# Fourier convolution slots cut into 30 ticks, with copies first on ScalarE, one more tap on TensorE and a split gelu

## Chip, cores and metric

The kernel runs on one core of a Trainium2 chip. The metric is the device time of one execution in microseconds. The whole network is one launch; the change touches one of its layers.

## The reference, cut to what matters

The network normalises and adds four layers in turn. The third, a Fourier convolution on an image of 2 x 64 x 256 x 256, is the one that matters here:

```python
x = jnp.einsum('bchw,oc->bohw', x, w_in)                      # 64 -> 384 channels
xf = jnp.fft.rfft2(patches_of_8x8(x)) * fft_filter
x = irfft2(xf)                                                # back to pixels
x = lax.conv_general_dilated(x, w_dw, padding=[(1, 1), (1, 1)], feature_group_count=C)   # 3x3, each channel alone
x1, x2 = jnp.split(x, 2, axis=1)
x = jax.nn.gelu(x1, approximate=False) * x2
return jnp.einsum('bchw,oc->bohw', x, w_out)                  # 192 -> 64 channels
```

Its result is added to its input (the residual).

## The kernel before, in words

**The work.** `fft_layer` (from line 1341) goes over 32 row blocks `r` of 8 image rows, and in each over the two images `b`: 64 **slots** `s = 2r + b`. The 384 channels lie in three blocks `oc` of 128, and a slot's 8 rows in two halves `h` of 4 rows, so the 3x3 convolution of a slot has six **units** `u = 3h + oc`, each 128 channels x 1024 pixels. The nine taps of a unit are shared out: TensorE adds the first one or two into a PSUM buffer `p_c` (two buffers, by the parity of the unit) with diagonal weights, VectorE adds the last five, one instruction each (line 1810), the fifth into `acc`, ScalarE multiplies the remaining ones into `ta` (line 1709), and GpSimd adds those to `acc` (line 1910). `N_PE = (1, 1, 2)` gives TensorE's number of taps by channel block; ScalarE has 3, 3 and 2, so 16 taps per slot.

**Around the units.** On TensorE, a row block is transposed (`turn`, 4 groups `g`), and each group brought to frequencies (`to_freq`), with ScalarE's copies `copy_ht` and `copy_ft` behind them; one PSUM buffer `p_q` serves these steps and the output products. For the next slot, `widen` (8 steps `p`) multiplies by `w_in` into the one buffer `p_f`, VectorE's `filter_` (line 1816) multiplies by the filter into one of two `v`, `from_freq` (16 steps `j`) brings it back to pixels in the one buffer `p_i`, and ScalarE's `place` (line 1688) copies that into `zb`, the padded image block. `widen(p)` waits for filter p - 1, `from_freq(j)` for filter j // 2 and for `place(j - 1)`. `carry` copies the two last rows of a block to the top of the next.

**Gate and output.** ScalarE's `gelu(s, h)` (lines 1719 and 1720) applies the gelu to channel block 0 and to half of block 2 into `ge`, once GpSimd has finished the sums of unit 3h + 2; GpSimd's `gate` (lines 1915 and 1919) multiplies them by the other channels; TensorE's `project` (two parts per slot) multiplies by `w_out`, and VectorE adds the residual (line 1832) and takes statistics for the next normalisation (line 1846). VectorE's last tap of a unit waits, before it overwrites `acc`, until the gate that read it is done.

**The order.** Each engine has its own program, written out by hand. TensorE and ScalarE go through 24 ticks per slot; tables such as `CONV_AT`, `BACK_AT` and `TURN_AT` say at which tick a step is issued. A tick is a place in the program, not a time: an engine executes in order and stands at the first wait that isn't met. VectorE goes through the slot's 30 taps and puts filters, residuals and statistics between them by `FILTER_N`, `RESIDUAL_N` and `STATS_N`. All turns and Fourier steps of the next row block lie in the slot with b = 0. GpSimd's order is: sums of unit 5 of the slot before, sums of unit 0, the gate of the slot before's second half, sums of units 1, 2, 3, gate of the first half, sums of unit 4. SyncE issues, in order and by row block, the load of the block after next, the store of the last one and the loads of its residual rows; the store waits for VectorE's residuals.

Of the kernel before, what the change touches and what calls it, by code (L numbers as in the profile page):

```python
# [1340 lines left out]
def fft_layer(nc, dram, bn2, bn3, H, W):  # L1341
# [3 lines left out]
    NR = H // P8  # L1345
# [11 lines left out]
    N_PE = (1, 1, 2)  # L1357
# [6 lines left out]
    with ExitStack() as ctx:  # L1364
# [53 lines left out]
        added = sem("act_tap_added")  # L1418
        ge_done = sem("gelu_done")
# [11 lines left out]
        def A(s, u):  # L1431

            n = [len(T_ACT[i % OC]) for i in range(6)]
            return s * sum(n) + sum(n[:u]) if s < NS else NS * sum(n) + (s - NS) * sum(n[:3]) + sum(n[:u])
# [88 lines left out]
        def _(pe):  # L1523
# [4 lines left out]
            def turn(r, g):  # L1528
                if g == 0:
                    pe.wait_ge(hn_done, r + 1)  # L1530
                    ahead(pe, xo_done, r * 4 - 4)
# [35 lines left out]

            def conv(s, b, u):

                h, oc = u // OC, u % OC  # L1570
                if u == 0:
                    if s < NS:
                        pe.wait_ge(zi_done, s * NJ + NJ)
                    else:
                        pe.wait_ge(edge, s - NS + 1)
                ahead(pe, tapped, (U(s, u) - 1) * ND)
                n = 2 if rows_of(s) == HR else 1
                for i in range(n):
                    rows = min(2, rows_of(s))
                    for t, (dy, dx) in enumerate(T_PE[oc]):  # L1580
                        y = h * HR + 2 * i + dy
                        last = nc.tensor.matmul(p_c[odd(s, u)][:, i * 512:i * 512 + rows * W], diag[:, oc, t, :],  # L1582
                                                zb[b][:, oc, y:y + rows, dx:dx + W],
                                                start=(t == 0), stop=(t == len(T_PE[oc]) - 1))
                last.then_inc(pc_ps, 1)
# [10 lines left out]
            def project(s, b, row, i):  # L1596
# [6 lines left out]
                if i == 0:  # L1603
                    pe.wait_ge(a_done, G(s, 0) + 1 if len(parts) == 2 or parts[0][1] == 0 else G(s - 1, 1) + 1)
                    if b == 0 and row is not None:
                        pe.wait_ge(q_done, (row + 1) * (2 * NG) + 2 * NG)
# [8 lines left out]
            def slot(r, b, s, first=False, no_next=False, no_row=False):  # L1615
                nb, ns = 1 - b, s + 1
                rows_left = r < NR - 1
                for j in range(TICKS):
                    if j in CONV_AT:
                        conv(s, b, CONV_AT[j])  # L1620
                    if not no_next and j in WIDEN_AT:
                        widen(ns, r + b, nb, WIDEN_AT[j])
                    if not first and j in PROJECT_AT:
                        project(s - 1, nb, r if rows_left else None, PROJECT_AT.index(j))
                    if not no_next:
                        if j in BACK_AT:
                            from_freq(ns, BACK_AT[j])
                        if j == NEXT_AT:
                            conv(ns, nb, 0)
                    if b == 0 and not no_row:  # L1630
                        if j in TURN_AT:
                            turn(r + 1, TURN_AT[j])
                        if j in FREQ_AT:
# [666 lines left out]
```

## Time and profile before

| | |
|---|---|
| three runs, median (lowest to highest) | 19279.74 us (19274.17 to 19281.36) |
| the profiled execution | 19279.87 us, its span 19278.1 us |
| VectorE busy, whole span | 18044.9 us, 94% |
| GpSimd busy | 17264.4 us, 90% |
| TensorE matmuls busy | 13115.2 us, 68% |
| ScalarE busy | 11279.7 us, 59% |
| VectorE's taps (line 1810), all | x1560 into `p_c`, mean 1274 ns; x390 into `acc` |
| GpSimd's additions (line 1910) | x1040, 2424.4 us, mean 2340 ns |
| ScalarE's taps (line 1709) | x1040, 1169.2 us, mean 1129 ns |
| TensorE's tap records (line 1582) | x2064, 993.2 us, mean 615 ns |
| ScalarE's copies into `zb` (line 1688) | x1024, 523.8 us, mean 512 ns |

The layer runs from about 15450 to 18890 us of the span; a longer Mamba layer lies before it and an 8x8 transform layer behind it. A busy time is the time in which an engine's instructions were in execution; the rest is waiting. A matmul of 512 float32 columns stands as two records in the trace. In the order of time, a bracket behind a row gives the idle time before it and what ended it.

### The profile page before, as it was taken

Reading aid. Unit: us, or ns where it says so; the run is one execution under the profiler, and the core shown is the slowest. Engines: PE = TensorE matmul, PEld = TensorE weight load, DVE = VectorE, ACT = ScalarE, POOL = GpSimd, SP = SyncE. Lnnn points to the kernel's source line nnn. Section 1 sums busy time; section 2 is a strip of 40 time slices with the busy share of each in tenths; the row PEclk is TensorE's granted clock in tenths of the full one; section 3 lists DMA queues with packets and bytes.
Section 4 is the critical chain, followed back from the end, with each engine's and each line's share of the span. In section 5 each row is a group of like instructions: output and inputs, shape, how many; then the busy total and the mean of one; then the engine's idle time right before and its main releaser. Section 6 shows DMA issues by size and latency. Waiting matters only on the chain. (4 is left out here: it accounts for less than half of the span.)

```text
span 19278.1 us, 147925 instructions
## 1 busy us (share of the span) xinstructions
PE 13115.2 (68%) x45790; PEld 4732.6 (25%) x45790; DVE 18044.9 (94%) x11642; ACT 11279.7 (59%) x12399; POOL 17264.4 (90%) x7417
## 2 busy tenths in 40 slices
PE   4876666666666666666666666666666678888885
PEld 2321111111111111111111111111111144444444
DVE  5989999999999999999999999999999979999996
ACT  1116666666666666666666666666666556666663
POOL 3989999999999999999999999999999969999991
PEclk8997777777777777777777777777777789999997
DMA  4335555555555555555555555555555511111114
GB/s 125 114 107 136 140 135 136 136 139 139 137 135 135 139 139 138 135 135 138 139 137 136 135 137 139 138 136 135 136 139 139 126 30 27 33 33 31 29 29 145
DMA packets 616198, 2249.23 MB, mean 117 GB/s; under 512 B 74881, under 2 KB 92147, under 8 KB 591091
## 3 DMA queue, kind: packets, MB, share of 16 engines
q1 hardware_dynamic: 610146, 2232.63, 44.9%
q10 hardware_dynamic: 5265, 7.14, 0.1%
q8 instruction: 368, 6.03, 0.1%
q14 instruction: 419, 3.43, 0.1%
HBM read 990.77 MB, written 174.96 MB: 60 GB/s over the span
## 5 line engine op out<-in xcount | busy, mean ns | idle before, releaser
L1324 POOL TENSOR_TENSOR h<-h,c_bc 128x1024 f32<-128x1024 f32 x4096 | 9603.0, 2357 | 791.6 <-DVE h L1280 746.2
L1280 DVE TENSOR_TENSOR_SCAN h<-da,state,px 128x1024 f32<-128x1024 f32 x3072 | 7210.1, 2347 | 109.6
L1151 ACT ACTIVATE da<-d_bc,a_neg 128x1024 f32<-128x1024 f32 x3072 | 3492.9, 1144 | 2615.9 <-DVE h L1280 2587.7
L1005 PE MATMUL py<-h,ysel 128*32 128x512 f32 x16384 | 2743.3, 802 | 2548.8 <-POOL h L1324 2548.5
L1274 DVE TENSOR_TENSOR px<-px,du_bc 128x1024 f32<-128x1024 f32 x3072 | 3783.7, 1232 | 312.6 <-PE px L991 89.1
L1910 POOL TENSOR_TENSOR acc<-acc,ta 128x1024 f32<-128x1024 f32 (+1 forms) x1040 | 2424.4, 2340 | 398.6 <-DVE acc L1810 295.4
L1316 POOL TENSOR_TENSOR xs<-du_bc,b_bc 128x1024 f32<-128x1024 f32 x1024 | 2409.9, 2353 | 0.0
L1280 DVE TENSOR_TENSOR_SCAN h<-px,state,xs 128x1024 f32<-128x1024 f32 x1024 | 2316.9, 2326 | 0.0
L1810 DVE SCALAR_TENSOR_TENSOR p_c<-zb,w_dw,p_c 128x1024 f32<-128x1024 f32 (+1 forms) x1560 | 1986.7, 1274 | 43.7 <-PE p_c L1582 11.2
L991 PE MATMUL px<-cf,bsel 32*128 32x512 f32 x3072 | 1335.6, 956 | 913.0 <-DVE h L1280 913.0
L1151 ACT ACTIVATE px<-d_bc,a_neg 128x1024 f32<-128x1024 f32 x1024 | 1144.2, 1117 | 894.4 <-DVE h L1280 880.1
L1005 PEld LDWEIGHTS py<-h,ysel 128*32 128x32 f32 x16384 | 509.8, 131 | 4376.6 <-POOL h L1324 3156.7
L1709 ACT ACTIVATE ta<-zb,w_dw 128x1024 f32<-128x1024 f32 (+1 forms) x1040 | 1169.2, 1129 | 302.8 <-POOL acc L1910 281.1
L1565 PE MATMUL p_i<-basis,v 128*128 128x128 f32 x6144 | 948.7, 291 | 437.4 <-ACT zb L1688 406.6
L962 PE MATMUL pm<-hx,w_tap 128*128 128x512 f32 x1024 | 765.8, 916 | 541.7 <-ACT hx L1072 541.7
L1582 PE MATMUL p_c<-zb,diag 128*128 128x512 f32 x2064 | 993.2, 615 | 150.2 <-DVE acc L1810 121.0
L674 POOL TENSOR_TENSOR apr<-apr 128x1024 f32<-128x1024 f32 x390 | 912.3, 2358 | 97.9 <-DVE apr L653 73.8
L1565 PEld LDWEIGHTS p_i<-basis,v 128*128 128x128 f32 x6144 | 777.2, 193 | 851.0 <-issue 550.9
L970 PE MATMUL pm<-hy,w_res 64*128 64x512 f32 x512 | 482.3, 1094 | 645.7 <-ACT u L1082 645.7
L1688 ACT ACTIVATE zb<-p_i 128x384 f32<-128x384 f32 x1024 | 523.8, 512 | 575.9 <-PE p_i L1565 564.3
L991 PEld LDWEIGHTS px<-cf,bsel 32*128 32x128 f32 x3072 | 329.4, 255 | 2029.0 <-issue 1409.7
L1112 ACT ACTIVATE yg<-pm,eps_c 128x1024 f32<-128x1024 f32 x256 | 285.1, 1114 | 919.3 <-PE pm L933 919.3
(219 smaller groups left out, 19476.1 us busy)
## 6 DMA issues: line engine op xcount, KB each, us to landing
d_bc<-delta SPq DMA_DIRECT2D x1024, 512.0 KB, 8.5
du_bc<-du SPq DMA_DIRECT2D x1024, 512.0 KB, 8.6
c_bc<-c_rows_dram SPq DMA_DIRECT2D x1024, 512.0 KB, 5.4
b_bc<-c_rows_dram SPq DMA_DIRECT2D x256, 512.0 KB, 8.1
hx<-x_dram SPq DMA_DIRECT2D x252, 256.5 KB, 6.3
st_x<-in_x_dram SPq DMA_DIRECT2D x32, 1024.0 KB, 4.9
ax<-in_x_dram SPq DMA_DIRECT2D x64, 512.0 KB, 3.4
xr<-x_dram SPq DMA_DIRECT2D x64, 512.0 KB, 6.1
```

The costliest lines, as they stand in the source:

```text
L991: last = nc.tensor.matmul(px[(t.par + q // 3 + q) % 2][:, cut], bsel[rows, q, :], cf[rows, cut], start=True, stop=True)
L1005: last = nc.tensor.matmul(py[32 * j:32 * j + 32, cut], ysel[:, :], h[:, (4 * q + j) % 8, cut], start=False, stop=(q == Q - 1))
L1151: nc.scalar.activation(out[:, :], d_bc[:, n % J, :], ACT.Exp, scale=a_neg[t.l][:, n:n + 1]).then_inc(da_done, 1)
L1274: nc.vector.tensor_tensor(out=x[:, :], in0=b[:, :], in1=du_bc[:, j, :], op=ALU.mult).then_inc(m1_done, 1)
L1280: nc.vector.tensor_tensor_scan(h[:, n % 8, PAD:T + PAD], a[:, :], x[:, :], state[:, 2 * t.l + t.b, n:n + 1], ALU.mult, ALU.add).then_inc(s ...
L1316: nc.gpsimd.tensor_tensor(out=xs[i][:, :], in0=du_bc[:, n % J, :], in1=b_bc[:, :], op=ALU.mult).then_inc(xs_done, 1)
L1324: nc.gpsimd.tensor_tensor(out=h[:, n % 8, 0:T], in0=h[:, n % 8, PAD:T + PAD], in1=c_bc[q % 2][:, :], op=ALU.mult).then_inc(m2_done, 1)
L1565: last = nc.tensor.matmul(p_i[:, c], v[j // 2 % 2][:, j % 2, c], basis[:, 1, :], start=True, stop=True)
L1582: last = nc.tensor.matmul(p_c[odd(s, u)][:, i * 512:i * 512 + rows * W], diag[:, oc, t, :], zb[b][:, oc, y:y + rows, dx:dx + W], start=(t ...
L1709: nc.scalar.activation(ta[odd(s, u)][t][:, 0:n * W].rearrange("p (y x) -> p y x", y=n), zb[b][:, oc, y:y + n, dx:dx + W], ACT.Identity, sc ...
L1810: nc.vector.scalar_tensor_tensor(out=out, in0=zb[b][:, oc, y:y + n, dx:dx + W], scalar=w_dw[:, oc, m:m + 1], in1=other, op0=ALU.mult, op1= ...
L1910: nc.gpsimd.tensor_tensor(out=acc[h][oc][:, c], in0=acc[h][oc][:, c], in1=ta[o][t][:, c], op=ALU.add).then_inc(added, 1)
```

## The change

The slot is cut into 30 ticks, one for each of VectorE's taps, and the tables are written anew. TensorE's tap matmuls are issued one at a time (`conv_piece`) between other steps instead of a unit at once. In a tick, ScalarE's `place` and the row block's copies now come ahead of its taps. `N_PE` is given by unit and TensorE takes a second tap for unit 4, which ScalarE and GpSimd give up (15 taps and additions per slot instead of 16). The gelu's two instructions are issued at two ticks, with a semaphore after the first that VectorE's tap into channel block 0 waits for instead of the gate. GpSimd's gate of the slot before stands behind the sums of unit 1 instead of unit 0. The fourth group of turn and Fourier step moves to the slot with b = 1. The core of the diff:

```diff
-    N_PE = (1, 1, 2)
+
+    N_PE = (1, 1, 2, 1, 2, 2)
...
-        TICKS = 24
-        CONV_AT = {4 * (u - 1) + 1: u for u in range(1, 6)}
-        NEXT_AT = 21
-        PROJECT_AT = (1, 4)
-        WIDEN_AT = {2 * p + 1: p for p in range(NP)}
-        BACK_AT = {j + 3: j for j in range(NJ)}
-        TURN_AT = {4 * g + 7: g for g in range(NG)}
-        FREQ_AT = {4 * g + 9: g for g in range(NG)}
-        CARRY_AT, GELU_BACK_AT, GELU_AT = 1, 5, 17
-        FILTER_N = {n: p for p, n in enumerate((3, 5, 8, 10, 13, 15, 18, 20))}
-        RESIDUAL_N, STATS_N = (3, 7), (4, 8)
+
+        TICKS = 6 * ND
+        CONV_AT = {0: (1, 0), 1: (1, 1), 5: (2, 0), 6: (2, 1), 7: (2, 2), 8: (2, 3), 10: (3, 0), 11: (3, 1),
+                   15: (4, 0), 16: (4, 1), 17: (4, 2), 18: (4, 3), 20: (5, 0), 21: (5, 1), 22: (5, 2), 23: (5, 3)}
+        NEXT_AT = 27
+        PROJECT_AT = (4, 9)
+        WIDEN_AT = {3 * p + 1: p for p in range(NP)}
+        BACK_AT = {3 * (j // 2) + 4 + j % 2: j for j in range(NJ)}
+
+        FIRST = 3
+        TURN_AT = ({13: 0, 19: 1, 25: 2}, {13: 3})
+        FREQ_AT = ({17: 0, 22: 1, 26: 2}, {16: 3})
+        TAP_AT = {2: (0, 0), 3: (0, 1), 4: (0, 2), 5: (1, 0), 6: (1, 1), 7: (1, 2), 9: (2, 0), 10: (2, 1), 14: (3, 0), 16: (3, 1),
+                  18: (3, 2), 21: (4, 0), 22: (4, 1), 26: (5, 0), 27: (5, 1)}
+        CARRY_AT, GELU_BACK_AT, GELU_AT = 1, (11, 12), (23, 24)
+        FILTER_N = {3 * p + 3: p for p in range(NP)}
+        RESIDUAL_N, STATS_N = (6, 12), (7, 13)
...
                 for j in range(TICKS):
-                    if j in CONV_AT:
-                        conv(s, b, CONV_AT[j])
                     if not no_next and j in WIDEN_AT:
                         widen(ns, r + b, nb, WIDEN_AT[j])
+                    if not no_next and j in BACK_AT:
+                        from_freq(ns, BACK_AT[j])
                     if not first and j in PROJECT_AT:
...
+                    if j in CONV_AT:
+                        conv_piece(s, b, *CONV_AT[j])
+                    if not no_next and j == NEXT_AT:
+                        conv(ns, nb, 0)
+                    if r < NR - 1 and j in TURN_AT[b]:
+                        turn(r + 1, TURN_AT[b][j])
+                    if r < NR - 1 and j in FREQ_AT[b]:
+                        to_freq(r + 1, FREQ_AT[b][j])
...
                 for j in range(TICKS):
-                    if j % 4 < NA:
-                        tap(s, b, j // 4, j % 4)
+                    if not no_next and j - 1 in BACK_AT:
+                        place(ns, nb, BACK_AT[j - 1])
+                    if r < NR - 1:
+                        if b == 0 and j == 0:
+                            norm(r + 1)
+                        if j - 1 in TURN_AT[b]:
+                            copy_ht(r + 1, TURN_AT[b][j - 1])
+                        if j - 1 in FREQ_AT[b]:
+                            copy_ft(r + 1, FREQ_AT[b][j - 1])
                     if not first and j == CARRY_AT:
                         carry(s - 1, nb)
...
+                    if j in TAP_AT:
+                        tap(s, b, *TAP_AT[j])
+                    if not first and j in GELU_BACK_AT:
+                        gelu(s - 1, 1, GELU_BACK_AT.index(j))
+                    if j in GELU_AT:
+                        gelu(s, 0, GELU_AT.index(j))
...
-                    ahead(dve, a_done, prev)
+
+                    ahead(dve, a_done if oc else ge_half, prev)
...
                 sums(s, 0)
+                sums(s, 1)
                 if not first:
                     gate(s - 1, 1)
-                for u in (1, 2, 3):
+                for u in (2, 3):
                     sums(s, u)
                 gate(s, 0)
                 sums(s, 4)
```

## Rows read from the trace of the kernel before

**Rows 1.** busy time by stretch: us, busy (x instructions), PEclk, DMA share, GB/s

```profile
17000.00:18000.00 1000.00, 829.06 (x4253) 453.30 (x4252) 919.70 (x821) 652.00 (x815) 918.89 (x391) 0.99 0.12 32
18728.00:18732.00 4.00, 3.60 (x4) 1.17 (x4) 3.93 (x4) 1.47 (x2) 3.71 (x3) 0.50 0.00 0
```

**Rows 2.** DVE's order of time (start us, us): the first taps of four slots

```profile
15555.97 3.94 DVE L1810 SCALAR_TENSOR_TENSOR p_c<-zb,w_dw,p_c 128x1024 f32<-128x1024 f32 x3 [8.44 <-PE p_c L1582]
...
17042.42 3.93 DVE L1810 SCALAR_TENSOR_TENSOR p_c<-zb,w_dw,p_c 128x1024 f32<-128x1024 f32 x3
...
17090.35 2.61 DVE L1810 SCALAR_TENSOR_TENSOR p_c<-zb,w_dw,p_c 128x1024 f32<-128x1024 f32 x2
...
18778.91 5.26 DVE L1810 SCALAR_TENSOR_TENSOR p_c<-zb,w_dw,p_c 128x1024 f32<-128x1024 f32 x4
```

**Rows 3.** waits, 15600 to 18800: us in total, times, longest

```profile
DVE v L1816 <- PE p_fr L1556: 206.9, 194, 1.6
...
POOL acc L1910 <- DVE acc L1810: 145.5, 62, 5.3
```

**Rows 4.** DVE's order of time, one stretch in detail

```profile
17035.92 5.26 DVE L1810 SCALAR_TENSOR_TENSOR p_c<-zb,w_dw,p_c 128x1024 f32<-128x1024 f32 x4
17041.22 1.28 DVE L1810 SCALAR_TENSOR_TENSOR acc<-zb,w_dw,p_c 128x1024 f32<-128x1024 f32 x1
...
17046.26 0.95 DVE L1816 TENSOR_TENSOR v<-p_fr,filt 128x768 f32<-128x768 f32 x1
17047.12 1.28 DVE L1810 SCALAR_TENSOR_TENSOR p_c<-zb,w_dw,p_c 128x1024 f32<-128x1024 f32 x1
17048.31 0.68 DVE L1832 TENSOR_TENSOR fxo<-p_qo,fxr 128x512 f32<-128x512 f32 x1
17048.91 1.27 DVE L1810 SCALAR_TENSOR_TENSOR acc<-zb,w_dw,p_c 128x1024 f32<-128x1024 f32 x1
```

**Rows 5.** POOL's order of time: gate products and additions

```profile
17034.61 2.37 POOL L1915 TENSOR_TENSOR ge<-ge,acc 128x1024 f32<-128x1024 f32 x1
...
17039.50 19.57 POOL L1910 TENSOR_TENSOR acc<-acc,ta 128x1024 f32<-128x1024 f32 x8
17059.02 2.37 POOL L1915 TENSOR_TENSOR ge<-ge,acc 128x1024 f32<-128x1024 f32 x1
```

**Rows 6.** ACT's order of time: first half of a gelu

```profile
17078.72 1.05 ACT L1719 ACTIVATE ge<-acc 128x1024 f32<-128x1024 f32 x1
```

**Rows 7.** PE's order of time, two stretches

```profile
17038.96 0.60 PE L1535 MATMUL p_qo<-f_mats,hn 128*128 128x128 f32 x4
17039.73 1.98 PE L1582 MATMUL p_c<-zb,diag 128*128 128x512 f32 x4 [0.17 <-ACT zb L1688]
17041.64 1.09 PE L1545 MATMUL p_qo<-basis,ht 128*64 128x128 f32 x16
...
17045.43 1.08 PE L1590 MATMUL p_qo<-ge,w_out 128*64 128x512 f32 x4
...
17047.44 0.92 PE L1556 MATMUL p_fr<-w_in,ft 64*128 64x384 f32 x4
...
17051.17 0.94 PE L1565 MATMUL p_i<-basis,v 128*128 128x128 f32 x6
17051.94 3.60 PE L1582 MATMUL p_c<-zb,diag 128*128 128x512 f32 x8
17055.47 0.92 PE L1556 MATMUL p_fr<-w_in,ft 64*128 64x384 f32 x4
17056.31 0.94 PE L1565 MATMUL p_i<-basis,v 128*128 128x128 f32 x6
17057.94 0.91 PE L1565 MATMUL p_i<-basis,v 128*128 128x128 f32 x6 [0.69 <-ACT zb L1688]
...
18728.40 3.78 PE L1582 MATMUL p_c<-zb,diag 128*128 128x512 f32 x4 [3.35 <-DVE acc L1810]
```

**Rows 8.** DMA issues, 15500 to 18800: KB each, median us to landing

```profile
fxr<-x_dram SPq DMA_DIRECT2D x62, 512.0 KB, 8.7
```

More of the change, by code:

```diff
@@ L1418, in fft_layer @@
         added = sem("act_tap_added")
+        ge_half = sem("gelu_first_half_done")
         ge_done = sem("gelu_done")
@@ L1431, in A @@
         def A(s, u):
-            n = [len(T_ACT[i % OC]) for i in range(6)]
+            n = [len(t) for t in T_ACT]
             return s * sum(n) + sum(n[:u]) if s < NS else NS * sum(n) + (s - NS) * sum(n[:3]) + sum(n[:u])
@@ L1530, in turn @@
                     pe.wait_ge(hn_done, r + 1)
-                    ahead(pe, xo_done, r * 4 - 4)
+                if g in (0, FIRST):
+                    ahead(pe, xo_done, r * 4 - 4 + (2 if g else 0))
                 ahead(pe, q_done, r * (2 * NG) + 2 * g)
@@ L1566, in from_freq, with conv_piece, pieces_of @@
                 last.then_inc(i_ps, 1)
-            def conv(s, b, u):
[L1570 to L1585, printed above, removed]
+            def conv_piece(s, b, u, k):
+                h, oc = u // OC, u % OC
+                if k == 0:
+                    if u == 0:
+                        if s < NS:
+                            pe.wait_ge(zi_done, s * NJ + NJ)
+                        else:
+                            pe.wait_ge(edge, s - NS + 1)
+                    ahead(pe, tapped, (U(s, u) - 1) * ND)
+                n = len(T_PE[u])
+                i, t = k // n, k % n
+                rows = min(2, rows_of(s))
+                dy, dx = T_PE[u][t]
+                y = h * HR + 2 * i + dy
+                last = nc.tensor.matmul(p_c[odd(s, u)][:, i * 512:i * 512 + rows * W], diag[:, oc, t, :],
+                                        zb[b][:, oc, y:y + rows, dx:dx + W], start=(t == 0), stop=(t == n - 1))
+                if k == pieces_of(s, u) - 1:
+                    last.then_inc(pc_ps, 1)
+            def pieces_of(s, u):
+                return len(T_PE[u]) * (2 if rows_of(s) == HR else 1)
+            def conv(s, b, u):
+                for k in range(pieces_of(s, u)):
+                    conv_piece(s, b, u, k)
             def product(parts, i, w):
@@ L1604, in project @@
                     pe.wait_ge(a_done, G(s, 0) + 1 if len(parts) == 2 or parts[0][1] == 0 else G(s - 1, 1) + 1)
-                    if b == 0 and row is not None:
-                        pe.wait_ge(q_done, (row + 1) * (2 * NG) + 2 * NG)
+                    if row is not None and (b or row < NR - 1):
+                        pe.wait_ge(q_done, row * (2 * NG) + 2 * NG if b else (row + 1) * (2 * NG) + 2 * FIRST)
                 ahead(pe, xo_done, O(s, i))
@@ L1648, in _ @@
                     slot(r, b, r * 2 + b)
-            slot(NR - 1, 0, NS - 2, no_row=True)
+            slot(NR - 1, 0, NS - 2)
             slot(NR - 1, 1, NS - 1, no_next=True)
@@ L1693, in tap @@
                 h, oc = u // OC, u % OC
-                if t >= len(T_ACT[oc]):
-                    return
                 if u == 0 and t == 0:
@@ L1760, in _ @@
                     slot(r, b, r * 2 + b)
-            slot(NR - 1, 0, NS - 2, no_row=True)
+            slot(NR - 1, 0, NS - 2)
             slot(NR - 1, 1, NS - 1, no_next=True)
             carry(NS - 1, 1)
-            gelu(NS - 1, 1)
+            for part in range(2):
+                gelu(NS - 1, 1, part)
             for b in range(2):
                 for u in range(OC):
-                    for t in range(NA):
+                    for t in range(len(T_ACT[u])):
                         tap(NS + b, b, u, t)
-                gelu(NS + b, 0)
+                for part in range(2):
+                    gelu(NS + b, 0, part)
         @block.vector
@@ L1784, in _ @@
             for oc in range(OC):
-                for t, tap in enumerate(T_PE[oc]):
+                for t, tap in enumerate(TAPS[:max(N_PE)]):
                     n = TAPS.index(tap)
@@ L1905, in sums @@
                 pool.wait_ge(tapped, (U(s, u) + 1) * ND)
-                for t in range(len(T_ACT[oc])):
+                for t in range(len(T_ACT[u])):
                     pool.wait_ge(t_done, A(s, u) + (t + 1))
```

56 lines of the change are left out of this document (17 added, 39 removed).

## The prediction, made before the changed kernel was built or run

> **What bounds the kernel now.** The change lies in the Fourier stage alone, so I read that stage. The table by stretch shows VectorE (DVE) and GpSimd (POOL) both busy 92% of the time there, with TensorE (PE) busy 83% and its granted clock at 0.99 of full speed [rows 1]. DVE's slots of 30 taps give the pace: 63 slots pass between the first tap and the first tap of the last slot, 3222.94 us or 51.16 each [rows 2]. A slot with b = 1 takes 47.93; the one with b = 0, which also turns the next row block into frequencies on PE, takes the rest of a pair, 54.4. The waits say where that goes: DVE waits 206.9 us for the widening matmul before a filter, about 3.3 per slot, and POOL 145.5 for DVE's last tap of a unit [rows 3]. So PE is late, not full: it stands in its program order, behind products, Fourier steps and pieces that themselves wait for a copy of ScalarE (ACT), while DVE stands still.
>
> **What each engine needs without waits.** DVE: four dependent taps take 5.30, so 1.325 each; a tap followed by something independent costs 1.19, a filter 0.86, a residual or a statistic 0.60 [rows 4]. Before, 12 of the 30 taps have an independent follower, so 14.3 + 18 x 1.325 + 8 x 0.86 + 4 x 0.60 = 47.4, which is the b = 1 slot less its short wait. After, filters stand before taps 3, 6, ... 24, residuals behind taps 6 and 12: 17 taps have such a follower, and the sum is 20.2 + 17.2 + 6.9 + 2.4 = 46.8 (-0.6). POOL: eight additions take 19.52, 2.44 each, a gate's two products 4.89 [rows 5]. Before, 16 additions and two gates are 48.8, more than DVE's 47.4: POOL alone would have capped any better order. Taking the second tap of unit 4 to PE removes one addition: 46.4. ACT, busy 65% [rows 1], loses one tap; splitting the gelu adds no instruction (two of 1.05 stay two [rows 6]), so both cost nothing by themselves. PE gains two pieces of 0.88 per slot, 1.8 us.
>
> **PE in the new order, by hand from the slot's first tap.** Prices from start to start [rows 7]: T (transpose) 0.77, F (to frequencies) 1.03 (its row 1.09 less the overlap), P (product) 2.01, W (widen) 0.84, B (back) 0.77 ahead of a piece and 0.86 elsewhere (its 0.94 less 0.08, the overlap that W shows with 0.92 and 0.84), C (tap piece) 3.53 / 4 = 0.88. Where a B has only its sibling's copy on ACT ahead of it, it starts 1.63 after that sibling. No row shows single pieces between other operations. From above one costs 0.96 (1.91 for two ahead of F, halved), from below I allow as much the other way, 0.80, since less weight of its own might be waited for; I take 0.88, the row with most pieces, and keep 0.08 x 14 = 1.1 us per slot, up or down, for the range.
> W1 can't start before filter 0, which starts at 3.84, has ended: 4.8. From there to the end of unit 5's pieces PE has, in order, 7 W (5.9), 14 B of which 11 run into a piece (10.9), 14 C (12.4), 2 P (4.0), and T and F once (1.8): 35.1. The chain of copies adds waits: with b = 1 I find 0.1 at B7, nothing where W or C lies between, and 0.8 at B11. So unit 5 is ready at 4.8 + 35.1 + 0.9 = 40.8, where DVE without waits would want it at 40.3 (tap 25). With b = 0 there is a second T and F before that point; T falls into B11's wait, F adds 1.0: 41.8. Everything earlier is in time: unit 2 at 15.3 for tap 10 at 16.1, W3 by 17.2 for the filter at 18.6, unit 4 at 31.6 for 32.3. Behind tap 25, B14, B15, T, F and the next slot's first pieces end at 47.9 for 48.3.
> So DVE waits 0.5 with b = 1 and 1.5 with b = 0: slots of 47.3 and 48.3, **95.6 us per pair**.
>
> **POOL's and ACT's queues.** Gelu's second half of the first part waits on ACT behind place 12, frequency copy and place 13, and is done at 43.3 with b = 0 and 41.6 with b = 1; POOL would reach its gate at about 40.7 and 41.4. It stands up to 2.6 us, and what is queued behind it, unit 4's sums, comes by 2.6 later into the next slot, where ACT's taps of unit 0 wait for them and place 0 stands behind those taps. In the next slot tap (0,2) then ends at 6.9, place 0 starts there, and B1, for which PE is free only at 8.6 (P), loses nothing. POOL's work of 46.4 fits into 47.3 with 0.9 over, so the delay is caught up. The back gate behind the second sums starts at about 24, its gelu is done at 22. DVE now needs only the first half of gelu for channel block 0 (tap 19): ready at 20.5, wanted at 31. The residual moves from taps 3 and 7 to 6 and 12; the store and the load of the next residual rows on SP's queue issue behind it, some 10 us later, and the load lands 8.7 us after its issue [rows 8], with 38 us until it is read: hidden. The other loads keep their place by row block. T3 and F3 move to the b = 1 slot, where their price is in the sum above; W6 reads them after they are copied.
>
> **Sum.** After: 63 slots at 47.8 = 3012, the first 1.3 less (no products, no backlog). Before: 3223. Gain 211 + 1 = 212 us. Two more diagonal weights are built once, under 1 us. The last slot has neither filters nor a next slot and the tail runs as before: nothing. The profiled execution took 19279.9, practically the median of the three runs (19279.7): 19280 - 212 = 19068; I say 19070.
>
> **A rule on the clock.** After PE stood 3.35 us idle ahead of a slot's second unit, four tap records took 3.78 us in some slots, where two pieces usually take 1.91 [rows 7]; in that stretch the granted clock is 0.50, which is 1.2 GHz [rows 1]. If the new order kept one such stretch in every pair and it fell on the path, 31 x 1.9 = 59 us would be added: 19130. The Trainium skill (TensorE: Matmul & The Clock Gate, "What's actually happening") says that the gate throttles after idleness and that activity releases it; the trace agrees. By that rule the new order, whose longest idle stretch of PE is some 2 us in my walk, would lose the slow stretches, and the sum stays at 19070.
>
> **The rivals.** (1) DVE's own time: if pieces cost 0.8 and no copy makes B wait, unit 5 is ready by 40.3 and each slot takes 46.8: 63 x 4.36 = 275, 19005 us. For it: my sum is over by only 0.5 with b = 1. Against it: F and T with b = 0. (2) PE dearer: at 0.96 a piece and a few more copy waits each slot has 1.1 to 2 us more, 48.9 to 49.8: 19140 to 19195. For it: PE would be busy nine tenths of the slot in strict order, so little absorbs it. (3) No change within 0.2%: PE must add 3 us to a slot, twice that. (4) Slower: the ring through POOL and ACT. Gate end, sums of unit 4 (4.9), ACT's taps (0,1) and (0,2) 2.1 (each about a gelu half), place 0, B1, PE's order up to B13, place 13, gelu's second half, gate (4.9). My steps give 48.5 for b = 0 and 46.1 for b = 1, 94.5 per pair, just under the forecast's 95.6; it closes first if ACT's taps stand ahead of copies. It decides beyond 95.6 and makes the kernel slower beyond 102.3, which needs 0.5 us for each of 8 pairs of B in both slots: 52 per slot, +53 us, 19333. For it: before, ACT's copies already wait in this way. Against: in the new order copies come first. That the change doesn't do what it says is unlikely: order and counts are fixed by hand.
>
> **Chances.** Forecast 0.5 (19030 to 19120), (1) 0.18, (2) 0.2, (3) 0.06, (4) 0.06. A measurement of this kernel can tell about 0.2% (39 us) from no change. The range takes in (1) and (2): 19000 to 19200. Faster 0.88, same 0.06, slower 0.06.
>
> **What would show it.** POOL's additions fall from 1040 by 64, PE's tap records rise from 2064 by 256. Right: DVE's waits for the widening matmul nearly gone, and instead a wait at tap 25 for the pieces of unit 5, about 0.5 and 1.5 us by turns; slots of 47.3 and 48.3; POOL's wait moved from DVE to gelu. Wrong: DVE waiting in several places of a slot, slots above 49, or no DVE wait at all and 46.8.

## The result, and the profile after

The changed kernel took 19105.06 us (median of four runs, 19099.55 to 19115.74), the kernel before 19279.95 beside it: a ratio of 0.9911, 95% interval 0.9896 to 0.9926. That is 175 us less where 210 were forecast, inside the range of 19000 to 19200. The profiled execution took 19099.55 us, its span 19097.7, which is 180.4 less than the span before.

The page of the changed kernel, its first part and three of its groups:

```profile
PE 13183.2 (69%) x46046; PEld 4686.6 (25%) x46046; DVE 17998.3 (94%) x11644; ACT 11214.6 (59%) x12335; POOL 17116.8 (90%) x7353
...
L1926 POOL TENSOR_TENSOR acc<-acc,ta 128x1024 f32<-128x1024 f32 (+1 forms) x976 | 2273.0, 2339 | 230.3 <-DVE acc L1826 135.8
...
L1826 DVE SCALAR_TENSOR_TENSOR p_c<-zb,w_dw,p_c 128x1024 f32<-128x1024 f32 (+1 forms) x1560 | 1983.2, 1271 | 135.7 <-PE p_c L1591 112.2
...
L1591 PE MATMUL p_c<-zb,diag 128*128 128x512 f32 x2320 | 1179.8, 607 | 115.8 <-DVE acc L1826 91.7
```

GpSimd's additions fell by 64 to 976, TensorE's tap records rose by 256 to 2320: the change does what it says. VectorE's busy time hardly moved (before 18044.9). What moved is its idle time. The stretches that answer to [rows 1], then the waits of the layer that answer to [rows 3]:

```profile
17000.00:18000.00 1000.00, 904.58 (x4510) 462.21 (x4510) 956.52 (x868) 665.35 (x833) 923.20 (x393) 0.99 0.13 33
17056.00:17060.00 4.00, 4.00 (x16) 1.64 (x14) 3.96 (x5) 2.64 (x4) 3.86 (x3) 0.57 0.00 0
```

```profile
POOL ge L1931 <- ACT ge L1733: 135.2, 69, 4.2
...
DVE p_c L1826 <- PE p_c L1591: 101.3, 73, 2.3
PE p_fr L1565 <- DVE v L1832: 100.8, 60, 1.7
POOL acc L1926 <- DVE acc L1826: 23.9, 3, 15.2
DVE v L1832 <- PE p_fr L1565: 2.5, 10, 0.3
```

VectorE is busy 957 us of 1000 instead of 919. Its 194 waits for the widening matmul, 206.9 us, have shrunk to 10 with 2.5 us; in their place it waits for tap pieces, 101.3 us. GpSimd's 145.5 us for VectorE have gone and it now waits 135.2 for the gelu. TensorE is busy 90% of the stretch, before 83%.

VectorE in order of time: the first taps of four slots, the filter 0 of one, and all its waits in two neighbouring slots (from 17001.35 with b = 0, from 17050.25 with b = 1):

```profile
15545.61 3.94 DVE L1826 SCALAR_TENSOR_TENSOR p_c<-zb,w_dw,p_c 128x1024 f32<-128x1024 f32 x3 [8.44 <-PE p_c L1591]
...
17001.35 3.93 DVE L1826 SCALAR_TENSOR_TENSOR p_c<-zb,w_dw,p_c 128x1024 f32<-128x1024 f32 x3
17005.19 0.95 DVE L1832 TENSOR_TENSOR v<-p_fr,filt 128x768 f32<-128x768 f32 x1
...
17043.75 5.26 DVE L1826 SCALAR_TENSOR_TENSOR p_c<-zb,w_dw,p_c 128x1024 f32<-128x1024 f32 x4 [2.05 <-PE p_c L1591]
...
17050.25 3.93 DVE L1826 SCALAR_TENSOR_TENSOR p_c<-zb,w_dw,p_c 128x1024 f32<-128x1024 f32 x3
...
17067.26 2.61 DVE L1826 SCALAR_TENSOR_TENSOR p_c<-zb,w_dw,p_c 128x1024 f32<-128x1024 f32 x2 [0.84 <-PE p_c L1591]
17070.13 0.96 DVE L1832 TENSOR_TENSOR v<-p_fr,filt 128x768 f32<-128x768 f32 x1 [0.26 <-PE p_fr L1565]
...
17093.01 5.26 DVE L1826 SCALAR_TENSOR_TENSOR p_c<-zb,w_dw,p_c 128x1024 f32<-128x1024 f32 x4 [1.13 <-PE p_c L1591]
...
18601.38 5.26 DVE L1826 SCALAR_TENSOR_TENSOR p_c<-zb,w_dw,p_c 128x1024 f32<-128x1024 f32 x4
```

The first slot with b = 0 takes 48.90 and waits once, 2.05 us at tap 25. An undisturbed slot with b = 1 takes 47.68 and waits 0.83 there: 96.58 us per pair. The slot at 17050.25 takes 49.26, because it also waits at tap 10 (unit 2) and at a filter. Ten of the 63 slots are such, each 1.6 us longer. The kernel before has ten long slots too, all with b = 0, mostly 55.48 against 53.96. From the first tap to the first tap of the last slot 3055.77 us pass (before 3222.94, [rows 2]), a gain of 167.2. The other 13.2 of the 180.4 lie outside the slots: the first tap comes 10.4 earlier, and from the last slot's first tap to the end 2.9 less pass. Most of the 10.4 is not the change's, as the paragraph on the sum shows.

### The profile page after: what moved, and what is told of

Its sections match the earlier page's. It is cut to its first block and busy times, and to the rows that moved or that the text cites. A ratio compares the mean times of both kernels' runs of the same rounds, so it can differ in the third digit from the quotient of the medians.

```text
span 19097.7 us, 148278 instructions
## 1 busy us (share of the span) xinstructions
PE 13183.2 (69%) x46046; PEld 4686.6 (25%) x46046; DVE 17998.3 (94%) x11644; ACT 11214.6 (59%) x12335; POOL 17116.8 (90%) x7353
## 5 line engine op out<-in xcount | busy, mean ns | idle before, releaser
L1926 POOL TENSOR_TENSOR acc<-acc,ta 128x1024 f32<-128x1024 f32 (+1 forms) x976 | 2273.0, 2339 | 230.3 <-DVE acc L1826 135.8
L1591 PE MATMUL p_c<-zb,diag 128*128 128x512 f32 x2320 | 1179.8, 607 | 115.8 <-DVE acc L1826 91.7
L1720 ACT ACTIVATE ta<-zb,w_dw 128x1024 f32<-128x1024 f32 (+1 forms) x976 | 1074.1, 1127 | 142.4 <-POOL acc L1926 120.5
```

Of the source, the lines that this page charges most:

```text
L1720: nc.scalar.activation(ta[odd(s, u)][t][:, 0:n * W].rearrange("p (y x) -> p y x", y=n), zb[b][:, oc, y:y + n, dx:dx + W], ACT.Identity, sc ...
L1926: nc.gpsimd.tensor_tensor(out=acc[h][oc][:, c], in0=acc[h][oc][:, c], in1=ta[o][t][:, c], op=ALU.add).then_inc(added, 1)
```

## The experiments

Each kernel starts from the changed one unless it says otherwise, and all compute the whole output. "Slots" are the intervals from a slot's first tap to the next slot's first tap, b = 1 and then b = 0, those that occur most; "in the slots" is the sum of all 63, to be held against the changed kernel's 3055.8. A slot is called disturbed when it is longer than most of its kind. The kernel before took 19281.24, 19274.01 and 19281.92 (medians of seven) beside the three groups of runs: so medians of one kernel differ by 8 us from group to group. A figure of one run is named as such.

**1. The first product one tick earlier.**

```diff
-        PROJECT_AT = (4, 9)
+        PROJECT_AT = (3, 9)
```

> The first product moves from tick 4 to tick 3, ahead of the second widening step. Theory A (the slot is set by PE's program from filter 0 to the pieces of unit 5; ahead of it PE stands idle for 1.68 us, waiting for that filter): the product fills the idle time and unit 5 is ready about 1.7 us earlier. DVE's wait at tap 25 falls from 0.83 to 0 with b = 1 and from 2.05 to about 0.4 with b = 0; undisturbed slots of 46.8 and 47.2 us instead of 47.68 and 48.90, and the slots that are 1.6 us longer because PE's clock halved become rarer. Time about 19010 to 19030. Theory B (the ring through POOL's gate, its sums, ACT's taps and the first copy sets the pair): pairs stay at 96.6 us, or fall at most to 94.5 and PE waits elsewhere; time 19040 to 19105.

Measured: 19081.01 (19077.37 to 19084.99), ratio 0.9898 (0.9881 to 0.9914). Undisturbed slots 47.43 and 48.65: the wait at tap 25 shrank by 0.25, not by the length of a product. TensorE, in order of time:

```profile
17021.77 1.13 PE L1591 MATMUL p_c<-zb,diag 128*128 128x512 f32 x2 [0.49 <-DVE acc L1826]
```

TensorE came earlier to unit 4's first piece and then stood there until VectorE had ended unit 2, whose `p_c` buffer unit 4 reuses. In the changed kernel that piece starts at 17026.08, 0.33 after VectorE could free the buffer (unit 2's last tap starts at 17024.41, and from such a tap's start to the piece behind it 1.34 pass elsewhere). So the stretch that sets the slot begins at unit 2's end, and only what lies behind it, up to unit 5's last piece, counts. In the slots 27.9 us went: 62 by 0.25 are 15.5, and the disturbed slots gave 12.4, as there are five instead of ten, and each is 0.7 to 0.9 longer instead of 1.6. The profiled executions differ by only 18.3, since here the first tap came at 15556.04, 10.4 later than in the changed kernel's, though nothing ahead of it differs. Theory A expected 46.8 and 47.2 and had missed this second start of the stretch.

**2. The tap back to ScalarE and GpSimd.**

```diff
-    N_PE = (1, 1, 2, 1, 2, 2)
+    N_PE = (1, 1, 2, 1, 1, 2)
...
-                   15: (4, 0), 16: (4, 1), 17: (4, 2), 18: (4, 3), 20: (5, 0), 21: (5, 1), 22: (5, 2), 23: (5, 3)}
+                   15: (4, 0), 16: (4, 1), 20: (5, 0), 21: (5, 1), 22: (5, 2), 23: (5, 3)}
...
-                  18: (3, 2), 21: (4, 0), 22: (4, 1), 26: (5, 0), 27: (5, 1)}
+                  18: (3, 2), 21: (4, 0), 22: (4, 1), 24: (4, 2), 26: (5, 0), 27: (5, 1)}
```

> The changed kernel with the second tap of unit 4 given back from PE to ACT and POOL; all else stays. PE has 1.8 us less work per slot, POOL 2.44 more. Theory A (POOL's own work would cap the new order without this part): the wait at tap 25 goes (PE is 1.8 us earlier), but POOL needs 48.8 per slot, plus what it waits for; slots of at least 48.8 by both parities, 97.7 per pair against 96.6, and DVE waits through ACT's late taps and copies. Time 19140 to 19170. Theory B (only PE's order mattered): slots of 47.0 to 47.4, time about 19050.

Measured: 19151.20 (one run), slots of 48.05 to 51.3, 49.0 on average, against GpSimd's own 48.8. Its additions stand there as x5 and x11 per slot with next to no idle time:

```profile
17010.26 12.22 POOL L1926 TENSOR_TENSOR acc<-acc,ta 128x1024 f32<-128x1024 f32 x5
17022.43 2.36 POOL L1931 TENSOR_TENSOR ge<-ge,acc 128x1024 f32<-128x1024 f32 x1
17024.87 2.37 POOL L1935 TENSOR_TENSOR ge<-ge,acc 64x1024 f32<-64x1024 f32 x1
17027.32 26.90 POOL L1926 TENSOR_TENSOR acc<-acc,ta 128x1024 f32<-128x1024 f32 x11
```

GpSimd is the bound in this order. The run is 46 us above the changed kernel, but 12 of the difference of the profiled executions lie ahead of the first tap, in work that is the same in both; in the slots the tap is worth 31.0 us, and behind the last slot's first tap 8.6 more, some 40 in all.

**3. The back gate ahead of unit 1's sums, as before.**

```diff
                 sums(s, 0)
-                sums(s, 1)
                 if not first:
                     gate(s - 1, 1)
-                for u in (2, 3):
+                for u in (1, 2, 3):
```

> The changed kernel with GpSimd's gate of the slot before in front of the sums of unit 1 again. Theory A (a ring: gate, all of POOL's sums up to unit 4, ACT's taps of unit 0, the first copy, PE up to the second product, the gelu, the gate again): 34.3 of POOL, 2.8 of ACT, 9.6 of PE, 4.5 of copies and gelu make 51.2 us, longer than the slot, so every slot takes about 51; time 19105 + 61 x 2.9 = about 19280, the place of the gate undoes the whole gain. Theory B (POOL has the slack to absorb a gelu 6 us late, since it is only moved in phase): slots stay at 47.7 and 48.9, time within 15 us of 19105.

Measured: 19486.47 (one run), slots 53.91 and 55.32, 381 us more. One round in order of time, GpSimd, ScalarE, VectorE:

```profile
17045.62 2.37 POOL L1931 TENSOR_TENSOR ge<-ge,acc 128x1024 f32<-128x1024 f32 x1 [5.58 <-ACT ge L1733]
```

```profile
17052.88 1.15 ACT L1720 ACTIVATE ta<-zb,w_dw 128x1024 f32<-128x1024 f32 x1 [5.33 <-POOL acc L1926]
```

```profile
17061.40 1.29 DVE L1826 SCALAR_TENSOR_TENSOR p_c<-zb,w_dw,p_c 128x1024 f32<-128x1024 f32 x1 [5.80 <-PE p_c L1591]
```

GpSimd stands for a gelu; its sums come late, so ScalarE's taps stand; the copies behind them come late, TensorE stands, and VectorE has no piece. ScalarE's waits for these sums, over the layer:

```profile
ACT ta L1720 <- POOL acc L1926: 459.4, 205, 5.3
```

The changed kernel has 117.6 there. The ring is real, and dearer than the 51 us per slot that I expected. Part of that is the clock: TensorE stands 4.78 us for a copy at 17054.58, the granted clock in 17052 to 17056 is 0.76, and nearly every slot has such a stretch. How much of the surplus it makes was not separated.

**4. Both halves of the gelu at one place.**

```diff
-                    if not first and j in GELU_BACK_AT:
-                        gelu(s - 1, 1, GELU_BACK_AT.index(j))
-                    if j in GELU_AT:
-                        gelu(s, 0, GELU_AT.index(j))
+                    if not first and j == GELU_BACK_AT[0]:
+                        for part in range(2):
+                            gelu(s - 1, 1, part)
+                    if j == GELU_AT[0]:
+                        for part in range(2):
+                            gelu(s, 0, part)
```

> The changed kernel with both halves of each gelu issued at the first half's tick. Theory A (the halves don't matter: what follows the gelu's end has slack or the copies lose about as much as the gate gains): the second half ends 0.5 us earlier in the tick of the copy of place 13, that copy starts up to 1 us later, DVE's wait at tap 25 grows by at most 0.5 us; time within 30 us of 19105. Theory B (the split is what keeps the copies in time): place 5 and place 13 come 1 us late, B6 and B14 with them, slots of 49.5 and more, time 19150 and above.

Measured: 19169.26 (one run), slots 49.26 and 49.49. Every slot with b = 1 but the first now has the slow stretch; TensorE in order of time and the same stretch in the table:

```profile
16996.31 1.65 PE L1565 MATMUL p_fr<-w_in,ft 64*128 64x384 f32 x4 [2.13 <-DVE v L1834]
16997.89 1.65 PE L1574 MATMUL p_i<-basis,v 128*128 128x128 f32 x6
```

```profile
16996.00:17000.00 4.00, 3.69 (x12) 2.15 (x14) 3.96 (x5) 0.43 (x2) 3.51 (x2) 0.57 0.00 0
```

In the slots 58.5 us are lost. Those with b = 1 are 1.58 longer than undisturbed ones of the changed kernel, exactly as its own disturbed ones (49.26), so what they lose is the clock's share. Those with b = 0 are 0.59 longer: a copy of ScalarE now lies behind both halves, and TensorE stands 1.62 us for it. The other 10.7 us of the profiled execution lie ahead of the first tap (15556.26). The number is Theory B's; its mechanism made the smaller part.

**5. The tap alone, on the kernel before.**

```diff
-    N_PE = (1, 1, 2)
+    N_PE = (1, 1, 2, 1, 2, 2)
```

(with the tables of taps by unit instead of by channel block)

> The kernel before, with its 24 ticks and its order, and with only one part of the change: PE takes the second tap of unit 4, ACT and POOL give it up. Theory A (in the old order PE is late and POOL is only near its limit, so the tap pays nothing alone): PE has 1.8 us more in its b = 0 slot, POOL's slack goes unused; time between 19260 and 19320. Theory B (POOL's 16 additions were what held the old order): 2.4 us per slot less, time about 19130.

Measured: 19372.98 (one run) against 19274.01, 99 us slower, and more than either theory allowed; 98.8 of it lie in the slots. GpSimd has less to do and gains nothing by it; TensorE's longer program makes the widening matmul later. The waits that answer to [rows 3]:

```profile
POOL acc L1910 <- DVE acc L1810: 383.8, 117, 7.6
...
DVE v L1816 <- PE p_fr L1556: 297.6, 237, 2.9
```

The same tap that saves some 40 us in the new order costs 99 in the old one.

**6. All four turns and Fourier steps in the slot with b = 0.**

```diff
-        FIRST = 3
-        TURN_AT = ({13: 0, 19: 1, 25: 2}, {13: 3})
-        FREQ_AT = ({17: 0, 22: 1, 26: 2}, {16: 3})
+        FIRST = 4
+        TURN_AT = ({13: 0, 17: 1, 20: 2, 24: 3}, {})
+        FREQ_AT = ({15: 0, 19: 1, 22: 2, 26: 3}, {})
```

> The changed kernel with the fourth turn and Fourier step back in the slot with b = 0 (turns at ticks 13, 17, 20, 24, Fourier steps at 15, 19, 22, 26). Theory A (the slot's length is set by what PE has to do between the first piece of unit 4, which waits for DVE's unit 2, and the last piece of unit 5): in b = 0 that stretch grows by 1.8 to 2.5 us, undisturbed slots of 50.7 to 51.4; in b = 1 it shrinks by 1.0, the wait of 0.83 at tap 25 goes, 46.9; pairs of 97.6 to 98.3 against 96.6, time 19135 to 19160. Theory B (PE's total per pair decides): pairs of 96.6, time 19105.

Measured: 19115.66 (one run), slots 46.77 and 49.87, 96.64 per pair against 96.58. With b = 1 VectorE then waits for nothing, and the slot with b = 0 pays it back; ten slots with b = 1 are 1.33 longer. In the slots it is 4.0 us more, and the first two slots with b = 0 alone are 6.5 longer. Where the fourth group lies is worth nothing that shows. Theory A's account still held: with b = 0, TensorE's time from unit 4's first piece to unit 5's last is 17.58 (17040.91 to 17058.49) against 16.61 (17026.08 to 17042.69), 0.97 more, and the slot is 0.97 longer. Its 50.7 to 51.4 were too high, since the turns between pieces cost 0.44 from start to start (17046.97 to 17047.41) instead of 0.77 and waits for copies went.

**7. ScalarE's copies behind its taps and gelus in each tick.**

```diff
-                    if not no_next and j - 1 in BACK_AT:
-                        place(ns, nb, BACK_AT[j - 1])
...
                     if j in GELU_AT:
                         gelu(s, 0, GELU_AT.index(j))
+                    if r < NR - 1:
...
+                    if not no_next and j - 1 in BACK_AT:
+                        place(ns, nb, BACK_AT[j - 1])
```

> The changed kernel with ACT's taps and gelus ahead of its copies in each tick, as before. Theory A (the copies are what PE waits for, so taps in front of them lengthen PE's chain): most places come 0.5 to 1.1 us later, and the first ones wait for POOL's sums as well; B steps wait more, DVE waits for widening steps or pieces in several places, slots of 50 and more, time 19230 or above. Theory B (ACT has enough idle time for either order): less than 0.3 us per slot, time within 20 us of 19105.

Measured: 19343.85 (one run), slots 49.85 and 52.88, or 51.43 and 54.46 where disturbed; VectorE's waits for tap pieces 284.2 us. Without copies first the new tables are slower than the kernel before. The copies are late by themselves and not through the ring, for ScalarE's taps hardly wait for GpSimd's sums here (the changed kernel has 117.6, experiment 3 459.4):

```profile
ACT ta L1720 <- POOL acc L1926: 1.4, 9, 0.2
```

TensorE's waits for copies into `zb` ahead of a `from_freq` grow from 89.9 to 216.4 us.

**8. Each unit's pieces together, at the place of the first.**

```diff
-                        conv_piece(s, b, *CONV_AT[j])
+                        if CONV_AT[j][1] == 0:
+                            conv(s, b, CONV_AT[j][0])
```

> The changed kernel with each unit's pieces issued together at the tick of the first one, as before, and all else as changed. Theory A (what counts is the stretch of PE's program up to unit 5's last piece): unit 5's four pieces come ahead of W7, B12, F1 and B13, so the wait at tap 25 goes; W7 comes about 1 us late for its filter instead; slots of 47.7 to 48.0 by both parities, about 95.8 per pair against 96.6, time about 19085. Theory B (single pieces between the other steps are what keeps the widening steps in time, as the kernel before shows with its waits for them): filters wait in several places, slots above 49, time above 19130.

Measured: 19334.36 (one run), slots 50.36 and 52.15, every other one with b = 1 53.55; VectorE waits 247.5 us for the widening matmul, as before the change. A whole unit is 3.5 us in front of a step that VectorE wants. This is Theory B. Part of the loss is the clock: TensorE's falls in almost every slot, and the 16 long ones, 3.2 us longer each, are those in which it stays low for longest (0.50 in 17072 to 17076 of one).

**9. Unit 5's pieces a tick earlier, the first product too, the second Fourier step a tick later.**

```diff
-                   15: (4, 0), 16: (4, 1), 17: (4, 2), 18: (4, 3), 20: (5, 0), 21: (5, 1), 22: (5, 2), 23: (5, 3)}
+                   15: (4, 0), 16: (4, 1), 17: (4, 2), 18: (4, 3), 19: (5, 0), 20: (5, 1), 21: (5, 2), 22: (5, 3)}
...
-        PROJECT_AT = (4, 9)
+        PROJECT_AT = (3, 9)
...
-        FREQ_AT = ({17: 0, 22: 1, 26: 2}, {16: 3})
+        FREQ_AT = ({17: 0, 23: 1, 26: 2}, {16: 3})
```

> The changed kernel with three edits to PE's order: the first product at tick 3, unit 5's pieces one tick earlier (19 to 22, so ahead of B11 and B13), and the second Fourier step of b = 0 at tick 23, behind the last of these pieces. Theory A (the stretch from unit 4's first piece to unit 5's last sets the slot; e1 gained only 0.25 us per slot since that first piece waits for DVE's unit 2 and not for PE): the stretch is 0.8 shorter with b = 1 and 1.8 with b = 0; with e1's gain the waits at tap 25 of 0.83 and 2.05 go, both slots take DVE's own 46.8 to 46.9; time 19105 - 63 x 1.4 = about 19015. Theory B (POOL's gate and the ring through ACT set the pair by then): PE's gain is given back as POOL's and ACT's waits, slots of 47.2 or more, time above 19035.

Measured: 19031.33 (19021.75 to 19031.72), ratio 0.9874 (0.9857 to 0.989): 74 us below the changed kernel. The only wait of VectorE in a pair of slots, and the total over the layer:

```profile
17011.62 3.94 DVE L1826 SCALAR_TENSOR_TENSOR p_c<-zb,w_dw,p_c 128x1024 f32<-128x1024 f32 x3 [0.93 <-PE p_c L1591]
```

```profile
DVE p_c L1826 <- PE p_c L1591: 30.7, 32, 1.4
```

The wait at tap 25 is gone, a pair takes 94.56, and no slot has a stretch of low clock. In the slots it is 78.5 us less: 62.6 from the waits and 16 from the disturbed slots. That lies between the two theories (19015, or above 19035), as the next slot's unit 0 kept a wait. 2 x 46.8 + 0.93 is 94.5: what is left is VectorE's own time and one wait for the next slot's unit 0.

**10. As 9, with the third Fourier step behind the next slot's unit 0.**

```diff
-        FREQ_AT = ({17: 0, 23: 1, 26: 2}, {16: 3})
+        FREQ_AT = ({17: 0, 23: 1, 28: 2}, {16: 3})
```

> e9 with one more edit: the third Fourier step of b = 0 goes from tick 26 to tick 28, behind the next slot's first pieces. e9 has one wait of DVE left, 1.04 us per pair, for these pieces. Theory A (it is the 1.03 us of this step): the wait goes, pairs of 93.5 us, which is DVE's own time; 31 x 1.04 = 32 us less than e9, 18990 to 19000. Theory B (POOL's and ACT's ring sets e9's 94.56 per pair, which is also the 94.5 of the prediction's sum for the ring): the wait moves elsewhere and the pair stays at 94.5, time 19020 to 19031.

Measured: 19062.89 (19052.87 to 19064.52), ratio 0.9886 (0.9869 to 0.9902), 31 us worse than 9; VectorE's wait grew to 2.31 in the slot read. TensorE in order of time there, and ScalarE:

```profile
17031.00 0.91 PE L1574 MATMUL p_i<-basis,v 128*128 128x128 f32 x6 [1.05 <-ACT zb L1701]
17032.82 3.41 PE L1591 MATMUL p_c<-zb,diag 128*128 128x512 f32 x4 [0.92 <-ACT zb L1701]
```

```profile
17037.52 0.60 ACT L1695 ACTIVATE ft<-p_qo 128x512 f32<-128x512 f32 x1 [3.73 <-PE p_qo L1554]
```

With the Fourier step gone from between them, TensorE stood twice for a copy, and its four records then took 3.41 us where they take 1.99 elsewhere. ScalarE, whose copy of that step stands ahead of its taps, waited 3.73. The step I took out had been filling a gap: in the nine slots with b = 0 that ran at full clock nothing was gained (47.74 against 47.78), and 21 others, with the clock low behind these waits (0.65 in 17032 to 17036), take 48.05 to 49.44, which is where the 31 us went. Neither theory had this.

**11. Three constant matmuls ahead of W1, in the idle time of 1.68 us.**

```diff
+                    if not first and j == 3:
+                        for _ in range(3):
+                            nc.tensor.matmul(p_i[:, 0:OC * 128], basis[:, 0, :], w_in[:, :], start=True, stop=True)
```

> The changed kernel with three more matmuls of 384 columns on PE per slot, at tick 3, into a buffer that the next step overwrites: they fill 1.2 of the 1.68 us for which PE stands idle ahead of the second widening step and delay nothing. Theory A (the ten slots that are 1.6 us longer come from PE's clock falling after that idle time): these slots vanish, the others stay at 47.68 and 48.90, about 16 us less in the stage. Theory B (the clock falls for another reason, so more PE work changes nothing, or costs): ten or so long slots remain.

Measured: 19110.54 (one run), slots 47.87 and 49.09, each 0.19 longer; eight long slots are left, all with b = 0. In one of them TensorE reads:

```profile
17004.58 1.13 PE L1591 MATMUL p_c<-zb,diag 128*128 128x512 f32 x2 [1.73 <-DVE acc L1829]
17005.64 1.47 PE L1565 MATMUL p_fr<-w_in,ft 64*128 64x384 f32 x4
17007.04 2.08 PE L1591 MATMUL p_c<-zb,diag 128*128 128x512 f32 x2
17008.91 2.29 PE L1636 MATMUL p_i<-w_in,basis 128*128 128x384 f32 x6
```

The slow stretch now begins ahead of the filler, behind the other idle time of the slot's start (1.73). With b = 1, where that one was 0.80 in the changed kernel, the long slots went from six to none; with b = 0, where it is 1.73, from four to eight. So the gap ahead of W1 had a part in the slow stretches; filling it alone removed six and brought four new ones.

**12. As 10, with the tap back.**

```diff
-    N_PE = (1, 1, 2, 1, 2, 2)
+    N_PE = (1, 1, 2, 1, 1, 2)
```

> e10 with the second tap of unit 4 given back to ACT and POOL. In this order PE has slack, so this is POOL's limit by itself. Theory A: POOL's 16 additions and 2 gates need 48.8 per slot and are never caught up; both slots take 48.8 to 49.2, time 18995 + 63 x 2.1 = about 19125. Theory B (e2's longer slots came from PE's and ACT's order and not from POOL's work): slots of 47 to 48, time below 19080.

Measured: 19178.88 (one run), slots 49.15 and 49.84, 49.4 on average: above GpSimd's 48.8 as in 2, and above what I expected, with waits of up to 3.3 us of VectorE's own. Nearly every slot has a stretch of half clock (0.50 in 17038 to 17042), so this run does not show GpSimd's limit by itself. As it starts from 10 and not from 9, what the tap is worth on 9 stays open.

## Why the prediction was right, and where its terms were off

**The bound.** "PE is late, not full" held: VectorE's busy time stayed, its idle time went, with TensorE busier than before. VectorE's own 46.8 us per slot was right: the one slot with a next slot but no further row block ahead took 46.76 with no wait. The start of the walk was right too: filter 0 at 3.84, W1 at 4.84 after the slot's first tap (17005.19 and 17006.19 against 17001.35), forecast 3.84 and 4.8.

**The price of a single piece.** This is the term that was too small. TensorE from W1 to the end of unit 5, b = 0, has 14 pieces; some of its rows:

```profile
17006.19 0.92 PE L1565 MATMUL p_fr<-w_in,ft 64*128 64x384 f32 x4 [1.68 <-DVE v L1832]
...
17014.12 1.02 PE L1591 MATMUL p_c<-zb,diag 128*128 128x512 f32 x2
17014.98 0.90 PE L1574 MATMUL p_i<-basis,v 128*128 128x128 f32 x6
17015.72 1.02 PE L1591 MATMUL p_c<-zb,diag 128*128 128x512 f32 x2
17016.68 1.08 PE L1606 MATMUL p_qo<-ge,w_out 128*64 128x512 f32 x4
...
17026.08 1.02 PE L1591 MATMUL p_c<-zb,diag 128*128 128x512 f32 x2
...
17032.23 1.13 PE L1591 MATMUL p_c<-zb,diag 128*128 128x512 f32 x2
17033.29 0.92 PE L1565 MATMUL p_fr<-w_in,ft 64*128 64x384 f32 x4
...
17042.69 1.02 PE L1591 MATMUL p_c<-zb,diag 128*128 128x512 f32 x2
```

From start to start a piece costs 0.86 ahead of a B, 0.96 ahead of a product, W or F, and 1.06 between F and W. The 14 take 13.1 instead of 12.4. (In the recorded sum 14 B are 11.05 and not 10.9, and 14 C 12.3; the total of 35.1 stands.) The stretch takes 37.56 (17006.19 to 17043.75) where 37.0 was forecast, so unit 5 is ready 42.4 after the slot's first tap instead of 41.8, and with b = 1 at about 41.2 instead of 40.8. VectorE wants it at 40.35, as forecast. Hence waits of 2.05 and 0.83 instead of 1.5 and 0.5, and 96.58 per pair instead of 95.6: 31 us over the layer. The upper bound of 0.96 that I had taken from two pieces ahead of F was nearly the mean (0.94); the row with most pieces was the one least like single pieces.

**Where the walk is anchored.** I started it at filter 0. Experiment 1 shows a second anchor the end of VectorE's unit 2, with 0.33 us between it and the piece that waits for it. It changed nothing in the forecast for this change, but in this order any saving ahead of it is worth 0.3 us at most; what lies behind it (experiment 9) counts in full.

**The clock.** The paragraph on it was the one that failed. I expected no slow stretch, since TensorE's longest idle time would be some 2 us. It is 1.7 us, and yet ten slots have one: in 17056 to 17060 the granted clock is 0.57, so most of that stretch ran at 1.2 GHz. TensorE there, to be held against the same steps at full clock (0.94 and 1.08):

```profile
17055.09 0.92 PE L1565 MATMUL p_fr<-w_in,ft 64*128 64x384 f32 x4 [1.68 <-DVE v L1832]
17055.94 1.41 PE L1574 MATMUL p_i<-basis,v 128*128 128x128 f32 x6
17057.28 1.98 PE L1606 MATMUL p_qo<-ge,w_out 128*64 128x512 f32 x4
```

Ten slots at 1.6 are 16 us, less than the 59 that I had set beside the sum. The kernel before lost as much: its ten long slots, some 15 us, are in the 3223 from which I subtracted, so the forecast had in effect booked their end as a gain. The slot at 17001.35 has the same 1.68 us of idle time there, and 1.73 ahead of it, and ran at full clock. The rule that I had drawn on (the Trainium skill, TensorE: Matmul & The Clock Gate, "What's actually happening") holds in its direction: each slow stretch read follows idle time. As I had used it, it names idleness and not which gap of a busy stream brings one; that 2 us would be short enough was my own guess, for which no row spoke.

**GpSimd and ScalarE.** The gate was forecast to stand up to 2.6 us for the gelu's second half; the trace has:

```profile
17045.14 2.37 POOL L1931 TENSOR_TENSOR ge<-ge,acc 128x1024 f32<-128x1024 f32 x1 [3.07 <-ACT ge L1733]
...
17093.82 2.36 POOL L1931 TENSOR_TENSOR ge<-ge,acc 128x1024 f32<-128x1024 f32 x1 [2.33 <-ACT ge L1733]
```

VectorE has no wait that follows from it in these two slots. GpSimd's cap of 48.8 with 16 additions is borne out by experiment 2.

**The sum.** Forecast 3011 us for the 63 slots, measured 3055.8: 31 from the pieces and waits, 16 from the clock, 2 less from the slot with no wait. Against these 45 us stand 13 gained outside the slots, of which I had forecast none. 9.2 of the 10.4 ahead of the first tap lie in the layer's start, which is the same work in both. Its granted clock, before and after:

```profile
15440.00:15560.00 120.00, 58.99 (x224) 38.40 (x224) 36.02 (x34) 24.04 (x33) 4.46 (x2) 0.52 0.14 44
```

```profile
15440.00:15560.00 120.00, 59.06 (x266) 36.82 (x268) 46.67 (x45) 28.58 (x40) 10.04 (x5) 0.64 0.14 44
```

From the layer's first instruction, a load of weights, to the first tap 106.8 us pass before (15449.15 to 15555.97) and 97.6 after (15448.01 to 15545.61). It is not the change: experiment 1, with the same start, took 105.9 at a granted clock of 0.53, and all others took 105.9 to 107.2 but two: 9 and 11 took 97.6 and 97.7, at 0.63. So these 9 us are luck of the profiled execution. How many of the other executions had them no trace says; without them it would have taken about 19109, 39 above the forecast, and still inside its range.

**The rivals.** DVE's own time (19005) fell; experiment 9 comes within 0.5 us per slot of it. "PE dearer" was half true, at 0.94 a piece, but gave 48.3 per slot, not 48.9. The slower case, the ring, did not close, and experiment 3 shows that the gate's place keeps it open, at 381 us. I had expected it to close first with ScalarE's taps ahead of its copies; experiment 7 does not show that, as its 239 us come without the wait for GpSimd's sums.

**The parts.** Undone alone, in one run each but compared with 19105.06: gate's place +381, copies first +239, single pieces +229, gelu in halves +64, the tap +46, the fourth Fourier group +11. These sum to 970 us for a change that brought 175: each part is worth what it is worth only beside the others. In the slots alone they are 379, 233, 222, 58, 31 and 4. All of these take in what the clock does in that run, which has up to one or two stretches of low clock in each slot where the changed kernel has eleven in all. The first half's own semaphore and the later residuals were not undone alone.

## What to carry to other kernels

When every engine follows a program of its own, look for the step that its consumer waits for and put what releases it (here a 0.5 us copy) ahead of bulk work on its engine, with long groups cut into pieces. Before moving a step earlier, find the last release that holds it (a buffer, a sum): only what lies behind that counts, and a step taken out may have been filling a gap. Price a piece by a row in which it has the neighbours that it will have, and test a transfer of work between engines in the order in which it will run: the same tap cost 99 us in one order and saved some 40 in the other. And before two kernels are compared to 10 us, compare the stretch that the change touches and not only the whole.

## What the runs showed of the hardware that was not expected

TensorE's clock fell to 1.2 GHz after idle time of only 1.7 to 2.1 us within a stretch in which it is busy 90%, in ten of 63 slots, while slots of the same kind with the same gaps ran at full clock. Which ones is no accident: counted from the first they are 1, 3, 8, 17, 22, 31, 36, 45, 50 and 59, so from the third on 9 and 5 slots apart by turns; what makes that pattern was not looked into. With 2.13 us (experiment 4) it fell in every slot with b = 1 but the first, after gaps of 1.05 and 0.92 close together (experiment 10) in 21 of 32 slots with b = 0, and with single gaps of up to 1.41 (experiment 9) in none. The layer's start was taken in one of two ways, with the same program: in 97.6 or 97.7 us at a granted clock of 0.63 or 0.64 (the changed kernel, experiments 9 and 11), or in 105.9 to 107.2 at 0.52 to 0.55 (the kernel before and the other experiments). Executions of one kernel lie 10 to 16 us apart here (19099.55 to 19115.74, 19021.75 to 19031.72); that this start is the cause is only argued, from the profiled executions, since no other execution has a trace.
